# Edge stages of a graph kernel: a third buffer for relation rows and one-hots, int16 types by transfer, the last 16 relation types in strips

## The reference, cut to what matters

```python
src, dst = (edge_index[0], edge_index[1])
m = x[src] * rel[edge_type]
m = jnp.concatenate([m[:half] @ W_in, m[half:] @ W_out], 0)
deg = jax.ops.segment_sum(jnp.ones((e,), x.dtype), dst, num_segments=n)
norm = 1.0 / jnp.maximum(deg, 1.0)
agg = jax.ops.segment_sum(m * norm[dst][:, None], dst, num_segments=n)
return jnp.tanh(agg + x @ W_loop + b)
```

## Time and profile before

| | |
|---|---|
| median of 3 runs | 2801.2 us |
| span of the profiled execution, its own time | 3183.3 us |
| TensorE matmul busy | 2759.1 us (87%) |
| weight load busy | 2587.3 us (81%) |
| VectorE busy | 2303.9 us (72%) |
| ScalarE busy | 1865.5 us (59%) |
| GpSimd busy | 1952.0 us (61%) |

### The profile page before, as it was taken

The page is one execution under the profiler, slowest core; times in us unless marked ns, Lnnn a source line. Parts: engine busy times, 40 slices in busy tenths (PEclk is TensorE's granted clock), DMA queues, the critical chain, the costliest instruction groups (busy, mean ns, idle before and its releaser), DMA issues. The chain is left out here.

```text
span 3183.3 us, 55393 instructions
## 1 busy us (share of the span) xinstructions
PE 2759.1 (87%) x20688; PEld 2587.3 (81%) x20688; DVE 2303.9 (72%) x3258; ACT 1865.5 (59%) x3179; POOL 1952.0 (61%) x2129
## 2 busy tenths in 40 slices
PE   4888888888888888797888888888888887997998
PEld 3888888888888888796877887878777786997998
DVE  6777777777677777896777777777777776995665
ACT  6556665555555555585555555555555554785444
POOL 6666666666666666455666666666666664892223
PEclk9999989999999999899999999999999999998999
DMA  8333333333333333353333333333333333452221
GB/s 259 119 90 89 89 89 90 89 89 90 88 89 90 90 88 90 92 164 104 90 90 90 89 90 92 88 90 90 89 89 92 88 90 98 136 158 90 69 67 64
DMA packets 162458, 312.57 MB, mean 98 GB/s; under 512 B 34061, under 2 KB 95309, under 8 KB 162229
## 3 DMA queue, kind: packets, MB, share of 16 engines
q0 software_dynamic: 79872, 218.21, 23.8%
q1 hardware_dynamic: 81120, 89.89, 8.8%
q10 hardware_dynamic: 1237, 1.41, 0.2%
HBM read 263.90 MB, written 45.48 MB: 97 GB/s over the span
## 5 line engine op out<-in xcount | busy, mean ns | idle before, releaser
L740 PE MATMUL edge_rg<-edge_rel_hi,edge_hot 128*128 128x256 f32 x6656 | 1551.7, 293 | 86.6 <-issue 63.0
L740 PE MATMUL edge_rg<-edge_rel_lo,edge_hot 128*128 128x256 f32 x4992 | 1312.3, 289 | 60.0 <-issue 58.9
L740 PEld LDWEIGHTS edge_rg<-edge_rel_hi,edge_hot 128*128 128x128 f32 x6656 | 1219.6, 197 | 143.7 <-issue 92.2
L548 ACT ACTIVATE edge_hot<-edge_typ,minus_type 128x512 fp32r<-128x512 f32 x832 | 526.8, 685 | 935.9 <-DMA dense_prev<-emb_t 383.9
L740 PEld LDWEIGHTS edge_rg<-edge_rel_lo,edge_hot 128*128 128x128 f32 x4992 | 983.1, 197 | 70.0 <-issue 68.5
L623 DVE TENSOR_TENSOR edge_m_lo<-edge_rg,edge_m_hi 128x1024 fp32r<-128x1024 f32 x416 | 509.3, 1224 | 241.3 <-ACT edge_m_hi L541 127.7
L604 DVE TENSOR_SCALAR edge_hot<-edge_typ,type_of 128x512 fp32r<-128x512 f32 x832 | 582.3, 741 | 12.4 <-ACT edge_hot L548 8.7
L753 PE MATMUL edge_small<-edge_m_hi,edge_sel 128*128 128x258 f32 x1664 | 458.1, 306 | 96.3 <-DVE edge_m_lo L623 90.7
L530 POOL DMA_INDIRECT edge_xg<-emb,src x416 | 399.0, 959 | 225.9 <-issue 96.2
L530 POOL DMA_INDIRECT work<-h,src x416 | 400.7, 963 | 221.9 <-issue 101.9
L530 POOL DMA_INDIRECT edge_xg<-h,src x416 | 400.2, 962 | 216.2 <-issue 102.8
(11 more groups left out here) (183 smaller groups left out, 3933.9 us busy)
## 6 DMA issues: line engine op xcount, KB each, us to landing
work<-emb,src POOLq DMA_INDIRECT x416
edge_xg<-emb,src POOLq DMA_INDIRECT x416
work<-h,src POOLq DMA_INDIRECT x416
edge_xg<-h,src POOLq DMA_INDIRECT x416
set_x_rows<-in_x SPq DMA_DIRECT2D x25, 256.0 KB, 3.9
emb<-set_e_rows SPq DMA_DIRECT2D x25, 256.0 KB, 2.9
emb_t<-acc SPq DMA_DIRECT2D x5, 1280.0 KB
dense_prev<-emb_t SPq DMA_DIRECT2D x25, 256.0 KB, 2.7
```

The costliest lines, as they stand in the source:

```text
L548: act.activation(hot[:, q % 2, c], typ[q % 2][:], ACT.Abs, bias=K["minus_type"][:, c:c + 1]).then_inc(distances, 1)
L740: ins = pe.matmul(rg[q % 2][:, t, :], hot[:, q % 2, c, t * P:(t + 1) * P], part[:, c, :], start=(c == 0 and part is rel_hi), stop=(c == FULL))
```

## The change

- `rg` and the one-hots get three buffers (`DEPTH`), chosen by g % 3, in the room of the two PSUM tiles `typ`.
- The types are turned to int16 once, in the setup, and stored in DRAM. For each group the sync queue loads them twice: broadcast to 128 partitions (`typ`, 1 KB each) and, for the strips, 256 bytes to each partition, tile t to partitions 32 t to 32 t + 31. TensorE's L723 goes.
- The fourth block of the one-hot becomes `hot_rest`, 128 columns wide instead of 512: one compare for all four tiles. Its relation table `rel_rest` has a copy for each tile, zero outside that tile's strip. The matmuls keep their number.
- TensorE's relation rows come with lag 0 instead of 2 and its sums with lag 3 instead of 4; the turned sums go between the second and the third tile of the relation rows. VectorE's and ScalarE's message parts have lag 3, and ScalarE does them first in its turn.
- The gather's first tile waits for the message of group g - 4, the other three still for the relation rows of group g - 2.
- The five stores of transposed rows move from the sync queue to ScalarE's.
- The node tables `dst` and `dst_rel` become int16, and a 512-column tile of zeros becomes one column read by broadcast.

```diff
-        rg = [s.ps(f"rg{b}", [P, GROUP, DIM]) for b in range(2)]
-        typ = [s.ps(f"typ{b}", [P, GROUP * P]) for b in range(2)]
+        rg = [s.ps(f"rg{b}", [P, GROUP, DIM]) for b in range(DEPTH)]
+        typ = s.sb("typ", [P, 2, GROUP * P], I16)
+        strips = s.sb("strips", [P, 2, P], I16)
+        hot = s.sb("hot", [P, DEPTH, FULL, GROUP * P], F32R)
+        hot_rest = s.sb("hot_rest", [P, DEPTH, P], F32R)
...
+            def load_types(g):
+
+                wait_past(sp, hot_done, g - 1)
+                wait_past(sp, distances, HOT_ACT * (g - 1))
+                of_group = types[g * GROUP * P:(g + 1) * GROUP * P]
+                sp.dma_start(typ[:, g % 2], of_group.partition_broadcast(P)).then_inc(types_in[g % 2], 16)
+                sp.dma_start(strips[:, g % 2],
+                             of_group.rearrange("(t e) -> t e", t=GROUP).unsqueeze(1).to_broadcast([GROUP, STRIP, P]))\
+                    .then_inc(types_in[g % 2], 16)
...
-                    if t < GROUP - 1:
-                        wait_past(pool, rel_tile, (GROUP - 1) * (g - 2) + t + 1)
+                    if t == 0:
+                        wait_past(pool, messages, g - 3)
+                    elif t < GROUP - 1:
+                        wait_past(pool, rel_tile, (GROUP - 2) * (g - 2) + t)
                     else:
                         wait_past(pool, rel_done, g - 1)
...
+                    act.wait_ge(messages, g + 1)
+                    if slot is of_three:
+                        wait_past(act, summed, g - 1)
+                    act.copy(m_hi[:, q % 2, :, 0:DIM], rg[slot(g, q)][:]).then_inc(hi_done, 1)
...
-                over_groups(act, (0, later(distance)), (2, high), (0, later(one_hot)), (3, copy_sums), (0, clear_one))
+                over_groups(act, (3, high(of_three)), (5, copy_sums), (0, later(distance(of_three))),
+                            (0, later(one_hot(of_three))), (3, clear_one))
...
+                    dve.wait_ge(types_in[q % 2], 32 * (2 * i + q // 2 + 1))
+                    for c in range(HOT_ACT, FULL):
+                        dve.tensor_scalar(hot[:, slot(g, q), c], typ[:, q % 2], K["type_of"][:, c:c + 1], None,
+                                          ALU.is_equal)
+                    dve.tensor_scalar(hot_rest[:, slot(g, q)], strips[:, q % 2], K["type_of"][:, FULL:], None,
+                                      ALU.is_equal).then_inc(hot_done, 1)
...
-                over_groups(dve, (2, message), (2, one_window), (4, add_window), (2, low), (0, one_hot_later))
+                over_groups(dve, (3, message(of_three)), (3, one_window), (3, low(of_three)), (6, add_window),
+                            (0, later(one_hot(of_three))))
...
+                    for t in range(GROUP):
+                        if between and t == GROUP // 2:
+                            between(g, q, i)
+                        for c in range(FULL):
+                            for part in (rel_hi, rel_lo):
+                                pe.matmul(rg[b][:, t, :], hot[:, b, c, t * P:(t + 1) * P], part[:, c, :],
+                                          start=(c == 0 and part is rel_hi), stop=False)
+                        ins = pe.matmul(rg[b][:, t, :], hot_rest[:, b, :], rel_rest[:, t, :], start=False, stop=True)
...
-                over_groups(pe, (4, one_window), (2, relation_rows), (0, spread_later), (4, turn_over))
+                over_groups(pe, (3, one_window), (0, relation_rows(of_three, turn_over_before)), (4, turn_over_last))
```

More of the change, by code:

```diff
@@ L22 @@
 I32 = mybir.dt.int32
+I16 = mybir.dt.int16
 U32 = mybir.dt.uint32
@@ L58 @@
 RCHUNKS = FULL + 1
-assert 0 < REST and 2 * REST <= P
+assert 0 < REST and 2 * REST == STRIP
 HID = 512
@@ L448, in phase_edges @@
         m_lo = s.sb("m_lo", [P, 2, GROUP, DIM], F32R)
+        rest_hi, rest_lo, rest_mix = (m_lo[:, 0, k] for k in range(3))
         sel = s.sb("sel", [P, GROUPS_IN_RING, GROUP * WIN + P - WIN], F32R)
@@ L582, in later @@
                 return run
-            distance(0, 0, 0)
-            one_hot(0, 0, 0)
+            distance(of_two)(0, 0, 0)
+            one_hot(of_two)(0, 0, 0)
+            if first:
+                act.wait_ge(rel_in, 16 * (1 + P // REST))
+                for at in range(0, CHUNKS, 5):
+                    chunks = slice(at, at + 5)
+                    act.dma_start(nodes_t[chunks].rearrange("c p f -> p c f"),
+                                  columns(K, chunks).rearrange("p c k n -> p c (k n)")).then_inc(columns_out, 16)
             widest = act.value_load(K["span"][0:1, 0:1], min_val=0, max_val=2 * FAR)
@@ new lines, in later, with run, message, stage @@
+            def later(stage):
+                def run(g, q, i):
+                    if not isinstance(g, int) or g > 0:
+                        stage(g, q, i)
+                return run
+            def message(slot):
+                def stage(g, q, i):
+                    at = slice(GROUP * (q % 2), GROUP * (q % 2 + 1))
+                    dve.wait_ge(gathered[q], 16 * GROUP * (i + 1))
+                    dve.wait_ge(rel_done, g + 1)
+                    dve.tensor_tensor(rg[slot(g, q)][:], xg[q // 2][:, at, :], rg[slot(g, q)][:],
+                                      ALU.mult).then_inc(messages, 1)
+                return stage
@@ L626, in select, with low, stage @@
+            def low(slot):
+                def stage(g, q, i):
+                    dve.wait_ge(hi_done, g + 1)
+                    dve.tensor_tensor(m_lo[:, q % 2], rg[slot(g, q)][:], m_hi[:, q % 2, :, 0:DIM].bitcast(F32),
+                                      ALU.subtract).then_inc(lo_done, 1)
+                return stage
             def select(out, dst):
@@ L715, in _ @@
         def _(pe):
-            def spread_types(g, q, i):
-                if isinstance(g, int):
-                    row = K["ident_r"][0:TYPE_ROWS, g // 2:g // 2 + 1].to_broadcast([TYPE_ROWS, P])
-                else:
-                    pe.wait_ge(picked, 2 * i + q // 2 + 1)
-                    row = pick[0:TYPE_ROWS, :]
-                pe.matmul(typ[q % 2][:], row, K["typ"][0:TYPE_ROWS, q % 2 * GROUP * P:(q % 2 + 1) * GROUP * P],
-                          start=True, stop=True).then_inc(typ_done, 1)
@@ L1584, in build @@
     h_t = nc.dram_tensor("h_t", [CHUNKS, P, DC * CHUNK], F32, kind="Internal").ap()
+    types = nc.dram_tensor("types", [TILES * P], I16, kind="Internal").ap()
     x2 = nc.dram_tensor("x2", [NODES_PAD, DIM], F32, kind="Internal").ap()
@@ L1610, in build @@
         keep("eps", [P, 2])
-        keep("zeros", [P, CHUNK, DC])
+        keep("zero", [P, 1])
+        keep("strip", [P, GROUP])
+        keep("part", [P, 2])
         keep("node_iota", [P, WIN])
```

243 lines of the change are left out of this document (129 added, 114 removed).

## The result

Over runs of the two kernels side by side the time after is 2830.21 us in the median (2828.86 to 2830.70), against 2801.01 (2799.98 to 2801.85) before: a ratio of 1.0102, with a 95% interval of 1.0087 to 1.0116. The change costs 29 us where 101 less were forecast. In the profiled execution the span is 2827.1 us. Ratios are of fast runs: a slow one of 3084.99 us, at a mean granted clock of 0.76 and among the twelve of the last experiment, is left out.

The account below looks back on a forecast made before the run. The prediction took TensorE and VectorE, not GpSimd, to bound the timed edge stages at 4.98 us a group. 2801.2 - 96 (L723) - 21 (third buffer, lags) + 15 (starts, ends) = 2699, said as 2700 us; range 2635 to 2830.

Parts of the forecast that it names:

- the choice of pace: Edge stages, timed runs at 4.98 us a group: either GpSimd sets this, or TensorE and VectorE do; the latter was forecast.
- the rival: Edge stages: GpSimd is and remains the pace, nothing gained but starts cost 15 us: 2795 to 2820; chance 0.15.
- The 689 us outside the edges: Rest of the kernel outside the two edge stages, 689 us of the 3183.3 us span, assumed kept in timed runs.
- 0.25 of coupling: TensorE's issue gaps in the edge stages, 0.25 us a group, bringing its turn from 4.66 to 4.91.
- 96 + 21 - 15 = 102 us: Whole kernel: 96 us from L723 leaving TensorE, 21 from third buffer and later lags, less 15 for starts and ends.
- The 0.05 for a third buffer: Edge turns: a third buffer and later lags win 0.05 us a group, or 21 us.
- The starts: Starts and ends of both layers: table behind types and mixing 2 x 4, stores 5, setup copies 2: 15 us lost.
- The lock: VectorE's SBUF compares delay gather issues, 0.18 us a turn, free in the forecast; as a slower rival, chance 0.16.
- the one with the lock: Edge stages: GpSimd is the pace and compares hold up its gathers: 2853, between 2835 and 2891; chance 0.16.
- VectorE's risk: Edge turns: each compare could wait up to 0.95 us for a running gather, two a turn up to 1.9.
- Types by transfer: Sync queue, each group: types land in 4 us, hidden; rival that they land late, 2887 us, chance 0.04.
- The profiled span: Profiled execution of the changed kernel: about 3190 us, 3150 to 3230, since GpSimd's stalls would stay.

Follow-up runs that it names:

- the last experiment: The kernel before with only its selection written as four 80-column compares with a sum: 2798.1 us, ratio 0.9988.
- the second profile: The kernel before, no edit, profiled once more: timed 2801.8 us, span 2800.0, without the GpSimd stalls of the profile that the prediction read.
- the gathers' cover gone: One gather of four left out from the fifth group on, in both kernels: before 2707.56 us (0.9668), after 2577.86 (0.9205).
- the last changed kernel: The changed kernel with both starts shortened, and compares and selection in the form with a sum: 2802.87 us, ratio 1.0000.

## Why the prediction was wrong

**The step that failed is the choice of pace.** "So either GpSimd is still the pace ... or TensorE and VectorE are": I took the second, at 0.62 (0.45 and 0.17) against 0.31 for GpSimd's pace (0.15 without the lock, 0.16 with it), because 4.98 us a group lay between 4.76 and 5.0 and a stalling GpSimd in the profile was taken for one that has room in the timed runs. Against the rival stood that "the stalls must all belong to the profiling and the pitch not at all"; just that is so. 4 x 1.2525 = 5.01 us a group is the pace of both kernels, the long gathers aside, and 4.98 was that number within its error. The 689 us outside the edges were right (691 in the second profile: 2800.0 - 1056.9 - 1052.4). Of 4.66, 4.76 and 5.0 the largest should have been taken: an engine that needs 5.0 us a group can't be run past at 4.98, and to have TensorE at the pace I had to add 0.25 of coupling, which only late gathers gave it: in the second profile L740 has no such gap from 600 to 1100 us.

**What TensorE and VectorE would give was near in size, and hidden.** Net of its starts it was forecast at 96 + 21 - 15 = 102 us; with the gathers' cover gone the change gives 129.7. It comes by another way than the sum, so the nearness is in part luck: there the kernel before turns at VectorE's 4.76 and the one after at TensorE's 4.43, where the sum began at a coupled 4.98 and took 0.23 and 0.05 from it. Those two turns themselves were read rightly. The 0.05 for a third buffer was not tried by itself.

**The starts were right as a sum**: 15 us, against 12.7 with the first gather's 0.4, and 14.4 with the longer waits up to 100.12. That is luck in part. Of the parts, 5 for the stores is near the 2.7 and up to 2.5 that came back without them; but two layers at 4 were put down to the types' place in the queue and the mixing, and the eight rest loads were not priced at all, though they hold the queue for 4.95 us.

**The lock was right as a mechanism and over-priced sixfold, and to say that it cost nothing was a part of the same failed step**, since GpSimd had no room. 0.18 us a turn were put down, and 12.2 us more in 408 turns are 0.030. It had 0.55 starts a turn within a compare; there were 0.22 long gathers a turn, and each lost 0.17 us instead of 0.33, because a gather that starts with the compare or in its last 0.13 us is not held. "It decides when the lock costs over 0.02 us a turn": it does cost more, and so the case came out slower, between the rival that kept GpSimd's pace (2795 to 2820) and the one with the lock (2835 to 2891). The row of the cast had more to tell: the compare was not the only holder, since the selection, already there, holds gathers too; in the kernel before the moments rarely met (11 times), and the change moved them.

The Trainium skill (SBUF — State Buffer, section "Who interferes with whom") says that VectorE shares a pair of ports with GpSimd: that a copy, cast or tensor-scalar from SBUF to SBUF may take it, that the form with an accumulator doesn't, that two inputs in SBUF contend with GpSimd's reads, and that one input in SBUF at the slow speed doesn't contend. By each of the four the trace agrees: 252 of 252, none of 500, 240 of 293, none of 2260. It also says that the one who comes first blocks the other fully, for its whole instruction. For a gather that comes second the trace nearly agrees, since it goes on 0.13 us before the instruction's end. I took the rule for VectorE's risk too, up to 1.9 us a turn. The compare by line (ns, least, median, most) shows how little it was:

```profile
L645 DVE TENSOR_SCALAR edge_hot<-edge_typ,type_of x416: 476/481/727, 63.8 to 2315.6; 128x512 fp32r<-128x512 int16 x139
```

At most 0.25 us longer, and 0.013 on average (494 against 481). 28 of them begin 0.47 to 0.70 us into a gather and take over 0.50, and all but one of these end 1.19 to 1.20 us after that gather's start, so such a compare is held until about 0.71 us into the gather and not for the whole of it; one that begins earlier in the gather takes its 0.48.

**Types by transfer** were hidden in the middle of the stages, as forecast: VectorE waits for them 10.1 us in all, three times, at the starts, and ScalarE 24.4 in five. One of these, the 5.98 us up to 94.43, was not hidden and is behind most of the 1.7 us above. (The rule on the strips' engines that the prediction draws from the Trainium skill stands on the page that it names, DMA: Bandwidth & Descriptors, but in the section "Why a DMA increments its semaphore by 16 and not by 1"; no run here shows on how many engines they went.) **Smaller sizes**: the compares take 0.48 and 0.28 (0.43 and 0.22 forecast), `distance` 720 ns instead of 629; both without effect. **The profiled span** was put at 3190 and came to 2827.1, since the stalls of the first profile belonged to that execution and not to the kernel.

What stays open: why the number of long gathers differs (89 to 146) between kernels with the same instructions in the middle of a stage. The moments at which landing gathers release VectorE's message, and thereby where the next ones meet it, would have to be followed; no run fixes them.

## What to carry to other kernels

Before a gain on one engine is counted, put the least turn of every engine side by side, issue gaps included, and take the largest, however busy the others look; leaving out a quarter of the suspected engine's work, in both kernels, settles it and shows what is hidden behind it. If a profiled execution is much longer than the timed runs, it needs a second profile before any pace is read from it. Where GpSimd's transfers are the pace, a VectorE compare or cast from SBUF to SBUF, or an instruction with both inputs in SBUF, can cost the kernel more than it saves VectorE: the slower form with a sum, in time that VectorE otherwise spends waiting, was worth 0.45% here.

## What the runs showed of the hardware

- A gather that starts within an instruction of VectorE from SBUF to SBUF (a compare or cast without a sum, or two SBUF inputs) and is held by it ends 0.81 to 0.82 us after that instruction's end, whether the instruction takes 0.48, 0.69 or 0.96 us; without it the gather takes 0.946.
- The other way, a compare of 0.48 us that begins 0.47 to 0.70 us into a gather ends 1.19 to 1.20 us after the gather's start, at most 0.25 us late; one that begins earlier in the gather isn't held.
- An indirect transfer of 128 rows costs 0.946 us of GpSimd and 0.305 until the next, the same with a wait in front of it or without, and with transfers at a share of 0.37 or 0.52. The traffic of the types did not slow its issue: the last changed kernel moves it too, and has the 0.946 and a pitch of 1.251.
- The form with a sum runs 512 columns of int16 in 738 ns instead of 481; four of 80 columns follow each other at 0.22 us (292 ns each).
